# Attention kernel on one Trainium2 core: pairs of heads taken together, queries and keys turned by DMA instead of TensorE

## Chip, cores and metric

The kernel runs on 1 core of one Trainium2 chip. The metric is device time in microseconds (us) of the whole program, lower is better. The kernel before took 1261.8 us, the median of 3 runs (1261.73 to 1263.38).

## What is computed

One transformer block over 32 batches of 256 tokens by 128 channels, all in 32-bit floats, cut to what matters:

```
xn  = layernorm(x)
h   = rmsnorm(xn) * norm_w
q, k, v = h @ Wq, split(h @ Wkv)              # 16 heads of 64
q, k = head_rmsnorm(q, q_gamma), head_rmsnorm(k, k_gamma)
sim = tanh(q @ k.T / 50) * 50 * 64**-0.5      # per batch and head, 256 x 256
o   = softmax(sim) @ v
out = x + o @ Wo + ffn(xn)   # ffn: 512 hidden, gelu; W1 and W2 each get a
                             # rank-4 update that is made from 16 rows of xn
```

## The kernel before

The work is a software pipeline over the 32 batches. A step n (of 36, from -2 to 33) does the attention of batch n and, beside it, other stages of its neighbours: "load" of batch n+3, "turn" of n+2 (layer norm, transpose of x), "front" of n+1 (projections, head norms), "back" of n-1 (output products), "store" of n-2. Each engine runs its own fixed list of operations in order; semaphores join them, nothing else does. A step has 16 slots, one for each head, and the tables `AUX`, `VECTOR_STEPS`, `POOL_STEPS` and `Y_PRODUCTS` say which further work an engine takes in which slot.

- **Scores.** In each even slot TensorE computes the scores of a pair of heads (`scores`, L481): 12 matmuls, two at a time on 64 rows of the array each, three products of 16-bit high and low parts. The two heads have one PSUM bank each (`ps_scores`). A pair may overwrite them when both tanh of the pair before are done (`clamp_done`).
- **Softmax.** ScalarE takes tanh of one head, 512 columns (L555), then exp of the head before (L563). GpSimd makes the low part of the exponentials (`lo_part`, L905). `RING = 4` heads are buffered.
- **Values.** TensorE multiplies by the values three slots later (`values`, L503 to L505, 12 matmuls a head), into `ps_o`; VectorE divides by the sum (`divide`, L702 and L706).
- **Everything else** goes through three PSUM banks, `ps_aux`, which are handed out strictly in the order of `AUX`: entry i uses bank i mod 3, and TensorE fills it when the reader of entry i-3 is done (`wait_bank`). Entries are the projections "q", "k", "v" (4 each a batch, three matmuls of 512 columns, L406 to L408), the transposes of x ("xhT", "xnT", L427), of the attention output ("oT", L455) and of the normalised queries and keys ("qkT", 8 a batch, 4 transposes each, L448), the two low-rank updates "low" (L461) and the hidden layer "hid" (L466).
- **Readers.** ScalarE squares q (L575), and VectorE then scales it with gamma and so frees the bank (L729). ScalarE copies k (L580), oT (L588), and takes gelu of hid (L596), which needs a table load before it and one before the next exp. Of v, ScalarE makes the high part (L585) and VectorE the low part, which frees the bank (L734). The same for qkT: high part L591, low part L738, into `heads_T`. VectorE makes `w_eff` from low (L746).
- **Head norms.** GpSimd squares k (L880), VectorE sums (L667) and makes a seed, GpSimd runs three Newton turns (L893 to L899), VectorE multiplies q and k by the result in four instructions (`normalise`, L694).
- **Output.** 24 products a batch accumulate in `ps_y` (L523, L525), placed by `Y_PRODUCTS`; VectorE adds the rest (L716).
- **DMA.** SyncE (SP) issues all transfers: x twice (L384, L388), the rows of xn for the update as six small DMAs (L375), and the result (L395).

## Time and profile before

| | |
|---|---|
| median of 3 runs | 1261.8 us |
| the profiled execution's own time | 1261.8 us |
| its span, first to last instruction | 1259.8 us |
| busy share TensorE / weight loads / VectorE / ScalarE / GpSimd | 93 / 77 / 82 / 86 / 73% |
| granted TensorE clock, mean | 0.992 |
| mean busy share of the 16 DMA engines | 5% |

An engine's busy time is the union of its instructions. Matmuls overlap (a values matmul is shown as 0.19 us but the next starts 0.03 us later), so what TensorE's work takes is read from start to start. The same holds, by less, for the other engines: a 512-column activation is shown as 0.6 us and the next starts after 0.5. The clock column is 1.00 at 2.4 GHz and 0.50 at 1.2 GHz.

### The profile page before, as it was taken

The numbers are of one execution on the slowest core, as the hardware profiler recorded it, in microseconds if no ns is written. First come the engines' busy times: TensorE is split into PE (matmuls) and PEld (weight loads), VectorE is DVE, ScalarE is ACT, GpSimd is POOL, SyncE is SP. The second block draws the span as 40 slices with busy tenths as digits, with TensorE's granted clock in tenths as the row PEclk, the third lists the DMA queues.
The fourth block names the chain that finished last, engine by engine and source line by source line (L and its number), as shares of the span: only waits on it lengthen the run. The fifth ranks groups of instructions, "written<-read, shape, count | busy, mean of one in ns | idle before, by whom it ended". The sixth has DMA issues, their size and how long they took to land.

```text
span 1259.8 us, 36165 instructions
## 1 busy us (share of the span) xinstructions
PE 1165.6 (93%) x13897; PEld 972.3 (77%) x13897; DVE 1032.2 (82%) x2153; ACT 1082.2 (86%) x2055; POOL 917.6 (73%) x1105
## 2 busy tenths in 40 slices
PE   3789999999999999999999999999999999999988
PEld 2468887778877778878778878778878778878777
DVE  6788889888889888889888889888889888888862
ACT  3589898889898889888888988888988888988885
POOL 4477777777777777877777877777777777777663
PEclk9899999999999999999999999999999999999999
DMA  4000000000000000000000000000000000000000
GB/s 132 10 11 11 14 16 7 15 15 11 15 15 7 15 15 11 15 15 7 15 15 11 14 16 7 15 15 11 14 15 7 15 15 15 10 11 11 11 6 9
DMA packets 32224, 19.41 MB, mean 15 GB/s; under 512 B 3508, under 2 KB 31288, under 8 KB 32056
## 3 DMA queue, kind: packets, MB, share of 16 engines
q1 hardware_dynamic: 32056, 17.12, 4.7%
q8 instruction: 112, 1.84, 0.6%
q14 instruction: 56, 0.46, 0.1%
HBM read 12.13 MB, written 4.19 MB: 13 GB/s over the span
## 4 chain that ended last, share of the span: by engine, by line
PE 42%; DVE 25%; ACT 19%; issue 11%; POOL 1%; ACTq 0%; POOLq 0%
PE ps_scores L481 8%; ACT probs L563 6%; PE ps_aux L455 5%; DVE qk L729 4%; PE ps_aux L448 4%; PE ps_aux L406 4%; PE ps_y L525 4%; DVE heads_T L738 3%; DVE sel_rows L760 3%; DVE qk L694 3%; PE ps_aux L408 3%; PE ps_aux L407 3%; ACT L596 3%; DVE norm L667 3%; ACT hid L596 3%
## 5 line engine op out<-in xcount | busy, mean ns | idle before, releaser
L905 POOL TENSOR_TENSOR probs_lo<-probs 128x512 f16<-128x512 f32 x512 | 586.3, 1150 | 235.1 <-ACT probs L563 232.9
L555 ACT ACTIVATE clamped<-ps_scores 128x512 f32<-128x512 f32 x512 | 310.3, 606 | 124.5 <-PE ps_scores L481 124.4
L563 ACT ACTIVATE probs<-clamped 128x512 f32<-128x512 f32 x512 | 324.9, 635 | 0.4
L503 PE MATMUL ps_o<-v_hi,probs 128*128 128x65 bf16 x2048 | 240.0, 195 | 4.5 <-DVE o_sb L706 2.7
L504 PE MATMUL ps_o<-v_lo,probs 128*128 128x64 bf16 x2048 | 239.2, 193 | 0.0
L505 PE MATMUL ps_o<-v_hi,probs_lo 128*128 128x65 bf16 x2048 | 238.9, 194 | 0.0
L481 PE MATMUL ps_scores<-heads_T 64*128 64x256 f16 x3072 | 212.9, 271 | 14.2 <-ACT clamped L555 14.0
L406 PE MATMUL ps_aux<-w_hi,xhT_hi 128*128 128x512 f32 x384 | 191.5, 499 | 31.9 <-DVE qk L729 21.6
L503 PEld LDWEIGHTS ps_o<-v_hi,probs 128*128 128x128 bf16 x2048 | 192.1, 99 | 30.1 <-issue 18.2
L504 PEld LDWEIGHTS ps_o<-v_lo,probs 128*128 128x128 bf16 x2048 | 189.8, 99 | 5.0
L505 PEld LDWEIGHTS ps_o<-v_hi,probs_lo 128*128 128x128 f16 x2048 | 190.2, 98 | 0.0
L738 DVE TENSOR_TENSOR heads_T<-ps_aux,heads_T 128x512 f16<-128x512 f32 x256 | 169.6, 683 | 14.9 <-ACT heads_T L591 14.5
L448 PE MATMUL ps_aux<-ident,qk 128*128 128x128 f32 x1024 | 151.6, 282 | 19.9 <-DVE qk L694 19.9
L694 DVE TENSOR_TENSOR qk<-qk,rnorm 128x1024 f32<-128x1024 f32 x128 | 167.6, 1309 | 2.1 <-POOL rnorm L899 2.1
L481 PEld LDWEIGHTS ps_scores<-heads_T 64*128 64x128 f16 x3072 | 131.8, 94 | 40.1 <-issue 17.6
L525 PE MATMUL ps_y<-wo_sb,oT 128*128 128x128 f32 x1024 | 160.5, 275 | 0.0
L734 DVE TENSOR_TENSOR v_lo<-ps_aux,v_hi 128x512 bf16<-128x512 f32 x128 | 87.8, 686 | 81.1 <-ACT v_hi L585 81.1
L408 PE MATMUL ps_aux<-w_hi,xhT_lo 128*128 128x512 f32 x384 | 152.8, 398 | 0.0
L407 PE MATMUL ps_aux<-w_lo,xhT_hi 128*128 128x512 f32 x384 | 152.8, 398 | 0.0
L591 ACT CAST heads_T<-ps_aux 128x512 f16<-128x512 f32 x256 | 145.1, 593 | 7.6 <-PE ps_aux L448 5.8
L448 PEld LDWEIGHTS ps_aux<-ident,qk 128*128 128x128 f32 x1024 | 115.0, 143 | 46.6 <-issue 42.1
L525 PEld LDWEIGHTS ps_y<-wo_sb,oT 128*128 128x128 f32 x1024 | 143.3, 191 | 7.4 <-issue 0.4
(83 smaller groups left out, 2211.2 us busy)
## 6 DMA issues: line engine op xcount, KB each, us to landing
x_in<-in_L_attn_tokens_dram SPq DMA_DIRECT2D x32, 128.0 KB, 2.3
x_res<-in_L_attn_tokens_dram SPq DMA_DIRECT2D x32, 128.0 KB, 2.3
out_dram<-y_sb SPq DMA_DIRECT2D x32, 128.0 KB, 1.9
sel_raw<-xn SPq DMA_DIRECT2D x192, 4.0 KB
qk<-in_L_attn_Wkv_dram SPq DMA_DIRECT2D x2, 512.0 KB, 5.4
qk<-in_L_attn_Wq_dram SPq DMA_DIRECT2D x1, 512.0 KB, 3.6
qk<-in_L_ffn_W_dram SPq DMA_DIRECT2D x2, 256.0 KB
hid<-in_L_attn_q_gamma_dram SPq DMA_DIRECT2D x1, 512.0 KB, 7.0
```

What stands on the lines that cost most here:

```text
L406: pe.matmul(o, hi_l, hi_r, start=True, stop=False)
L448: ins = pe.transpose(bank[:, (j * TT + t) * P:(j * TT + t + 1) * P], qk[:, par, t, at:at + P], ident[:])
L481: ins = pe.matmul(ps_scores[:, odd, t * seq:(t + 1) * seq], heads_T[rows, pair, left, k, keys], heads_T[rows, pair, right, q], start=(i == ...
L503: pe.matmul(full, hi[:, col], v_hi[:, par, u, h], start=(u == 0), stop=False)
L504: pe.matmul(full[:, 0:DH], hi[:, col], v_lo[:, par, u, h], start=False, stop=False)
L505: ins = pe.matmul(full, probs_lo[:, buf, col], v_hi[:, par, u, h], start=False, stop=(u == TT - 1))
L525: ins = pe.matmul(o, oT[:, pair, tok], wo_sb[:, pair], start=False, stop=(i == n - 1))
L555: nc.scalar.activation(clamped[:, buf], ps_scores[:, s % SCORE_BANKS], ACT.Tanh).then_inc(clamp_done, 1)
L563: nc.scalar.activation(probs[:, buf], clamped[:, buf], ACT.Exp, bias=LIFT, scale=SOFTCLAMP * DH ** -0.5).then_inc(probs_done, 1)
L694: v.tensor_tensor(part, part, r.unsqueeze(3).to_broadcast([P, 2 * TT, 4, DH]), ALU.mult)\
L738: v.tensor_tensor(heads_T[:, k, 1].rearrange("p j t -> p (j t)"), bank, heads_T[:, k, 0].rearrange("p j t -> p (j t)"), ALU.subtract)\
L905: g.tensor_tensor(probs_lo[:, buf], probs[:, buf], probs[:, buf].bitcast(BF16)[:, 1::2], ALU.subtract).then_inc(lo_made, 1)
```

## The change

A step now has 8 slots, one for each pair of heads.

- `tanh`, `exp` and `lo_part` each take a whole pair, 1024 columns, in one instruction. `RING` is 2 pairs; `clamped` holds one pair. `values` of both heads comes two slots after their scores, ahead of the slot's other products instead of behind them.
- The "qkT" entries leave `AUX`: no transposes of q and k on TensorE, and no reads of their results. Instead ScalarE writes the 16-bit high part of a quarter of the normalised q and k (`half`, 1024 columns, from SBUF), VectorE the low part (`halves`, 1024 columns, two inputs in SBUF), and SP issues a transposing DMA for each (`turn_heads`), 256 KB, two for each of four chunks: 8 a batch. The scores of pairs 2c and 2c+1 wait for chunk c. `heads_T` has one buffer, `halves16` two.
- "xhT" and "xnT" become one entry "xT". Projections q and k of a batch are begun one step earlier (stage "turn" instead of "front"), the layer norm's statistics too.
- All orders are new: `AUX` has 21 entries, and ScalarE gets a list of its own, `SCALAR_STEPS`.
- SP's list: select rows in slot 1, store in slot 2, chunk 3 of the current batch in slot 3, chunks 0, 1, 2 of the next one in slots 5, 6, 7.

```diff
@@ -49,73 +49,63 @@
 
 AUX_BANKS = 3
 AUX = [
-    (1, "k", 0, 1), (1, "k", 1, 1), (1, "q", 2, 1),
-    (2, "qkT", 4, 0), (2, "qkT", 5, 0),
-    (3, "q", 3, 1),
-    (4, "oT", 0, -1), (4, "oT", 1, -1), (4, "k", 2, 1),
-    (5, "k", 3, 1), (5, "low", 0, 0), (5, "v", 0, 1),
-    (6, "oT", 2, -1), (6, "v", 1, 1),
-    (7, "oT", 3, -1), (7, "qkT", 6, 0),
-    (8, "qkT", 7, 0), (8, "v", 2, 1),
-    (9, "hid", 0, 0), (9, "hid", 1, 0),
-    (10, "low", 1, 0), (10, "v", 3, 1),
-    (11, "xhT", 0, 2),
-    (12, "qkT", 0, 1), (12, "qkT", 1, 1),
-    (13, "xnT", 0, 2),
-    (14, "q", 0, 2), (14, "qkT", 2, 1),
-    (15, "qkT", 3, 1), (15, "q", 1, 2),
+    (0, "k", 2, 1), (0, "k", 3, 1), (0, "oT", 0, -1),
+    (1, "v", 0, 1), (1, "v", 1, 1), (1, "oT", 1, -1),
+    (2, "low", 0, 0), (2, "v", 2, 1), (2, "v", 3, 1), (2, "oT", 2, -1),
+    (3, "xT", 0, 2), (3, "low", 1, 0), (3, "oT", 3, -1),
+    (4, "q", 0, 2), (4, "q", 1, 2),
+    (5, "hid", 0, 0), (5, "hid", 1, 0),
+    (6, "k", 0, 2), (6, "k", 1, 2),
+    (7, "q", 2, 2), (7, "q", 3, 2),
...
-RING = 4
-VALUES_LAG = 3
+RING = 2
+VALUES_LAG = 2
...
+SCALAR_STEPS = [
+    [("tanh",), ("q", 3, 1), ("exp",), ("k", 2, 1), ("k", 3, 1)],
+    [("tanh",), ("half", 3, 0), ("exp",), ("oT", 0, -1), ("v", 0, 1), ("v", 1, 1)],
+    [("tanh",), ("oT", 1, -1), ("exp",), ("v", 2, 1), ("v", 3, 1)],
+    [("tanh",), ("oT", 2, -1), ("exp",), ("xT", 0, 2)],
+    [("tanh",), ("oT", 3, -1), ("exp",), ("q", 0, 2), ("q", 1, 2)],
+    [("tanh",), ("half", 0, 1), ("exp",), ("hid", 0, 0), ("hid", 1, 0)],
+    [("tanh",), ("half", 1, 1), ("exp",), ("k", 0, 2), ("k", 1, 2)],
+    [("tanh",), ("half", 2, 1), ("exp",), ("q", 2, 2)],
+]
 VECTOR_STEPS = [
+    [("q", 2, 1), ("divide",), ("result",), ("q", 3, 1), ("sum", 2, 1), ("sum", 3, 1), ("sum", 4, 1)],
+    [("sum", 5, 1), ("norm_apply",), ("divide",), ("v", 0, 1), ("v", 1, 1)],
+    [("sum", 6, 1), ("sum", 7, 1), ("seed",), ("divide",), ("v", 2, 1), ("v", 3, 1)],
+    [("low", 0, 0), ("halves", 3, 0), ("divide",), ("low", 1, 0)],
+    [("xT", 0, 2), ("select",), ("divide",), ("normalise", 0, 1)],
+    [("q", 0, 2), ("q", 1, 2), ("divide",), ("normalise", 1, 1), ("halves", 0, 1)],
+    [("sum", 0, 2), ("sum", 1, 2), ("divide",), ("normalise", 2, 1), ("halves", 1, 1)],
+    [("normalise", 3, 1), ("divide",), ("norm_stats",), ("halves", 2, 1)],
 ]
 POOL_STEPS = [
+    [("rstd",), ("lo",)],
+    [("square", 2, 1), ("square", 3, 1), ("lo",)],
+    [("newton", 0), ("lo",)],
+    [("newton", 1), ("newton", 2), ("lo",)],
+    [("bias",), ("lo",)],
     [("lo",)],
...
+    [("square", 0, 2), ("square", 1, 2), ("lo",)],
 ]
+TURN_STEPS = {3: (3, 0), 5: (0, 1), 6: (1, 1), 7: (2, 1)}
+SELECT_SLOT = 1
+STORE_SLOT = 2
+Y_PRODUCTS = {2: 2, 3: 5, 4: 4, 5: 3, 6: 5, 7: 5}
...
+        halves16 = sb("halves16", [P, 2, 2, PAIRS // CHUNKS, TT * 2, P], F16)
+        heads_T = sb("heads_T", [P, 2, PAIRS, TT, 2, P], F16)
-        clamped = sb("clamped", [P, RING, TT * seq])
-        probs = sb("probs", [P, RING, TT * seq])
-        probs_lo = sb("probs_lo", [P, RING, TT * seq], F16)
+        clamped = sb("clamped", [P, 2, TT * seq])
+        probs = sb("probs", [P, RING, 2, TT * seq])
+        probs_lo = sb("probs_lo", [P, RING, 2, TT * seq], F16)
...
+        def chunk_of(par, c):
+
+            return qk[:, par].rearrange("p t (j n) -> p (t j) n", j=2)[:, :, c * 4 * DH:(c + 1) * 4 * DH]\
+                .rearrange("p b (a n) -> p a b n", n=P)
...
+            def turn_heads(st, c, ahead):
+
+                b, _, _ = st.batch(ahead)
+                wait(sp, scores_done, 2 * PAIRS * (b - 1) + 4 * c + 4)
+                for half, made in enumerate((half_hi_made, half_lo_made)):
+                    sp.wait_ge(made, CHUNKS * b + c + 1)
+                    sp.dma_start(heads_T[:, half, 2 * c:2 * c + 2].rearrange("p a t j n -> p (a t j) n"),
+                                 halves16[:, c % 2, half].rearrange("p a b n -> p (a b n)"),
+                                 transpose=True).then_inc(heads_turned[c], 16)
...
-                elif kind == "qkT":
-
-                    if k % 2 == 0:
-                        wait(pe, qk_normed, 4 * b + k // 2 + 1)
-                    for j in range(2):
-                        for t in range(TT):
-                            at = j * HEADS * DH + k * P
-                            ins = pe.transpose(bank[:, (j * TT + t) * P:(j * TT + t + 1) * P],
-                                               qk[:, par, t, at:at + P], ident[:])
...
             def scores(st, pair):
 
                 b, par, _ = st.batch(0)
-                wait(pe, qkT_split, PAIRS * b + pair + 1)
-                wait(pe, clamp_done, HEADS * b + 2 * pair)
+                if pair % 2 == 0:
+                    wait(pe, heads_turned[pair // 2], 32 * (b + 1))
+                wait(pe, clamp_done, PAIRS * b + pair)
                 hi, lo, q, k = 0, 1, 0, 1
                 for t in range(TT):
-                    keys = slice(t * P, (t + 1) * P)
                     for i, (left, right) in enumerate(((hi, hi), (lo, hi), (hi, lo))):
                         for odd in range(2):
                             rows = slice(DH * odd, DH * odd + DH)
                             ins = pe.matmul(ps_scores[:, odd, t * seq:(t + 1) * seq],
-                                            heads_T[rows, pair, left, k, keys], heads_T[rows, pair, right, q],
+                                            heads_T[rows, left, pair, t, k], heads_T[rows, right, pair, :, q],
                                             start=(i == 0), stop=(i == 2))
...
+            def values(st, ahead, pair):
...
-                        col = slice(u * seq + t * P, u * seq + (t + 1) * P)
-                        pe.matmul(full, hi[:, col], v_hi[:, par, u, h], start=(u == 0), stop=False)
-                        pe.matmul(full[:, 0:DH], hi[:, col], v_lo[:, par, u, h], start=False, stop=False)
-                        ins = pe.matmul(full, probs_lo[:, buf, col], v_hi[:, par, u, h],
...
-                    if "attn" in st.stages and s % 2 == 0:
-                        scores(st, s // 2)
-                    for task in aux_tasks(st, s, PER_BATCH):
+                for s in range(PAIRS):
+                    if "attn" in st.stages:
+                        scores(st, s)
+                    late = pair_of(st, s, VALUES_LAG)
+                    if late:
+                        values(st, *late)
+                    for task in aux_tasks(st, s):
                         aux(st, *task)
                     if "back" in st.stages and s in Y_PRODUCTS:
                         result(st, sum(Y_PRODUCTS.get(i, 0) for i in range(s)), Y_PRODUCTS[s])
...
+            def tanh(st, pair):
+                b, _, _ = st.batch(0)
+                wait(act, scores_done, 2 * PAIRS * b + 2 * pair + 2)
+                wait(act, probs_done, PAIRS * b + pair)
+                nc.scalar.activation(clamped[:].rearrange("p j n -> p (j n)"),
+                                     ps_scores[:].rearrange("p j n -> p (j n)"), ACT.Tanh).then_inc(clamp_done, 1)
+
+            def exp(st, pair):
+                b, _, _ = st.batch(0)
+                wait(act, clamp_done, PAIRS * b + pair + 1)
+                wait(act, attended, PAIRS * b + pair + 1 - RING)
+                nc.scalar.activation(probs[:, pair % RING].rearrange("p j n -> p (j n)"),
+                                     clamped[:].rearrange("p j n -> p (j n)"), ACT.Exp, bias=LIFT,
+                                     scale=SOFTCLAMP * DH ** -0.5).then_inc(probs_done, 1)
+
+            def half(st, c, ahead):
+                b, par, _ = st.batch(ahead)
+                act.wait_ge(qk_normed, CHUNKS * b + c + 1)
+                wait(act, heads_turned[(c + 2) % CHUNKS], 32 * (b + c // 2))
+                nc.scalar.copy(halves16[:, c % 2, 0], chunk_of(par, c)).then_inc(half_hi_made, 1)
...
+            def halves(st, c, ahead):
+
+                b, par, _ = st.batch(ahead)
+                dve.wait_ge(half_hi_made, CHUNKS * b + c + 1)
+                v.tensor_tensor(halves16[:, c % 2, 1], chunk_of(par, c), halves16[:, c % 2, 0], ALU.subtract)\
+                    .then_inc(half_lo_made, 1)
...
+            def lo_part(st, pair):
+                b, _, _ = st.batch(0)
+                buf = pair % RING
+                pool.wait_ge(probs_done, PAIRS * b + pair + 1)
+                g.tensor_tensor(probs_lo[:, buf].rearrange("p j n -> p (j n)"), probs[:, buf].rearrange("p j n -> p (j n)"),
+                                probs[:, buf].rearrange("p j n -> p (j n)").bitcast(BF16)[:, 1::2],
                                 ALU.subtract).then_inc(lo_made, 1)
 
```

In `AUX` and the lists the last number is the batch relative to the step's. Entry by entry the banks of the new `AUX` are: slot 0 k2, k3, oT0 in banks 0, 1, 2; slot 1 v0, v1, oT1 in 0, 1, 2; slot 2 low0, v2, v3, oT2 in 0, 1, 2, 0; slot 3 xT, low1, oT3 in 1, 2, 0; slot 4 q0, q1 in 1, 2; slot 5 hid0, hid1 in 0, 1; slot 6 k0, k1 in 2, 0; slot 7 q2, q3 in 1, 2.

## Rows read from the trace of the kernel before

**Rows 1.** The page's first part: busy time of each engine, its share of the span, instructions.

```profile
PE 1165.6 (93%) x13897; PEld 972.3 (77%) x13897; DVE 1032.2 (82%) x2153; ACT 1082.2 (86%) x2055; POOL 917.6 (73%) x1105
```

**Rows 2.** Timeline of GpSimd, its once-a-batch addition: start us, us, instruction.

```profile
134.38 1.72 POOL L912 TENSOR_TENSOR x_b<-x_res,b_bc 128x256 f32<-128x256 f32 x1
...
1151.89 1.72 POOL L912 TENSOR_TENSOR x_b<-x_res,b_bc 128x256 f32<-128x256 f32 x1
```

**Rows 3.** Groups by line: count | busy us, mean ns | idle before, releaser.

```profile
L905 POOL TENSOR_TENSOR probs_lo<-probs 128x512 f16<-128x512 f32 x512 | 586.3, 1150 | 235.1 <-ACT probs L563 232.9
L563 ACT ACTIVATE probs<-clamped 128x512 f32<-128x512 f32 x512 | 324.9, 635 | 0.4
L555 ACT ACTIVATE clamped<-ps_scores 128x512 f32<-128x512 f32 x512 | 310.3, 606 | 124.5 <-PE ps_scores L481 124.4
...
L694 DVE TENSOR_TENSOR qk<-qk,rnorm 128x1024 f32<-128x1024 f32 x128 | 167.6, 1309 | 2.1 <-POOL rnorm L899 2.1
...
L746 DVE SCALAR_TENSOR_TENSOR w_eff<-ps_aux,scale_col,w1T 128x512 f32<-128x512 f32 x32 | 23.7, 742 | 0.3 <-PE ps_aux L461 0.3
...
L603 ACT CAST w_hi<-qk 128x1024 fp32r<-128x1024 f32 x3 | 3.0, 1044 | 5.6 <-DVE qk L824 5.6
```

**Rows 4.** Timeline of TensorE in one step: start us, us, instruction.

```profile
608.48 0.50 PE L406 MATMUL ps_aux<-w_hi,xhT_hi 128*128 128x512 f32 x1
...
609.29 0.60 PE L448 MATMUL ps_aux<-ident,qk 128*128 128x128 f32 x4
609.72 0.39 PE L525 MATMUL ps_y<-wo_sb,oT 128*128 128x128 f32 x2
609.95 0.19 PE L503 MATMUL ps_o<-v_hi,probs 128*128 128x65 bf16 x1
...
610.31 0.63 PE L448 MATMUL ps_aux<-ident,qk 128*128 128x128 f32 x4
...
616.75 0.83 PE L481 MATMUL ps_scores<-heads_T 64*128 64x256 f16 x12
617.51 1.09 PE L448 MATMUL ps_aux<-ident,qk 128*128 128x128 f32 x8
```

**Rows 5.** Timeline of ScalarE around the gelu of one step.

```profile
633.57 0.62 ACT L555 ACTIVATE clamped<-ps_scores 128x512 f32<-128x512 f32 x1
634.05 0.65 ACT L563 ACTIVATE probs<-clamped 128x512 f32<-128x512 f32 x1
634.72 1.28 ACT L596 ACT_TABLE_LOAD   x1
636.02 1.57 ACT L596 ACTIVATE hid<-ps_aux,b_col 128x256 f32<-128x256 f32 x4
637.53 0.60 ACT L555 ACTIVATE clamped<-ps_scores 128x512 f32<-128x512 f32 x1
```

**Rows 6.** Timeline of VectorE in one step.

```profile
618.80 0.68 DVE L729 TENSOR_TENSOR qk<-ps_aux,g_bc 128x512 f32<-128x512 f32 x1
619.40 1.28 DVE L738 TENSOR_TENSOR heads_T<-ps_aux,heads_T 128x512 f16<-128x512 f32 x2
```

**Rows 7.** TensorE by stretches: length, busy (x), PEclk, DMA share, GB/s.

```profile
70.00:75.00 5.00, 3.89 (x58) 1.00 0.18 52
75.00:79.00 4.00, 2.80 (x24) 0.71 0.00 0
```

**Rows 8.** Timeline of TensorE inside the second of those stretches.

```profile
75.67 0.83 PE L481 MATMUL ps_scores<-heads_T 64*128 64x256 f16 x12 [1.78 <-ACT clamped L555]
77.03 1.94 PE L448 MATMUL ps_aux<-ident,qk 128*128 128x128 f32 x8 [0.53 <-DVE qk L694]
```

**Rows 9.** Timeline of SP: the issue of the six small row DMAs of one step.

```profile
613.15 3.99 SPq L375 DMA_DIRECT2D sel_raw<-xn  x6
```

**Rows 10.** DMA issues: KB each, median us from issue to landing.

```profile
x_in<-in_L_attn_tokens_dram SPq DMA_DIRECT2D x32, 128.0 KB, 2.3
qk<-in_L_attn_Wq_dram SPq DMA_DIRECT2D x1, 512.0 KB, 3.6
```

More of the change, by code:

```diff
@@ L288, in block_kernel @@
         v_split = sem("v_split")
-        qkT_hi_made = sem("qkT_hi_made")
-        qkT_split = sem("qkT_split")
+        half_hi_made = sem("half_hi_made")
+        half_lo_made = sem("half_lo_made")
+        heads_turned = [sem(f"heads_turned{c}") for c in range(CHUNKS)]
         oT_copied = sem("oT_copied")
@@ L322, in wait_bank, with aux_tasks, bank_of, pair_of @@
                     return
[L324 removed]
+        def aux_tasks(st, slot):
             for i, (s, kind, k, ahead) in enumerate(AUX):
[L326 removed]
+                if s == slot and STAGE[ahead] in st.stages:
                     yield i, kind, k, ahead
[L329 to L331 removed]
+        def bank_of(kind, k):
+            i = [(what, n) for _, what, n, _ in AUX].index((kind, k))
+            return ps_aux[:, i % AUX_BANKS, :]
+        def pair_of(st, slot, lag):
+            ahead, pair = (0, slot - lag) if slot >= lag else (-1, slot - lag + PAIRS)
             there = "attn" if ahead == 0 else "back"
[L333 removed]
+            return (ahead, pair) if there in st.stages else None
+        def chunk_of(par, c):
+            return qk[:, par].rearrange("p t (j n) -> p (t j) n", j=2)[:, :, c * 4 * DH:(c + 1) * 4 * DH]\
+                .rearrange("p b (a n) -> p a b n", n=P)
         def run_all(eng, run):
@@ new lines, in run @@
+            def run(st):
+                for s in range(PAIRS):
+                    for what, *k in SCALAR_STEPS[s]:
+                        if what == "tanh":
+                            if "attn" in st.stages:
+                                tanh(st, s)
+                        elif what == "exp":
+                            if "attn" in st.stages:
+                                exp(st, s)
+                        elif STAGE[k[1]] in st.stages:
+                            if what == "half":
+                                half(st, *k)
+                            else:
+                                aux(st, what, *k)
@@ L616, in _, with norm_stats @@
             v.memset(v_hi[:, :, :, :, DH:DH + 1], 1.0)
-            def norm_stats(st):
-                b, par, half = st.batch(2)
+            def norm_stats(st, ahead):
+                b, par, half = st.batch(ahead)
                 dve.wait_ge(x_loaded[par], 16 * (half + 1))
@@ L726, in aux @@
                     if k == 0:
-                        wait(dve, aux_filled["qkT"], PAIRS * (b - 1))
+                        wait(dve, half_hi_made, CHUNKS * (b - 1))
                     t, c = k // 2, k % 2
@@ L872, in _, with square @@
             pool.wait_ge(masks_made, 6)
-            def square(st, k):
-                b, par, _ = st.batch(1)
+            def square(st, k, ahead):
+                b, par, _ = st.batch(ahead)
                 t, c = k // 2, 2 + k % 2
```

306 lines of the change are left out of this document (121 added, 185 removed).

## The prediction

> **What bounds the kernel now.** The page's first part comes first: TensorE is busy for 93% of the span, and no other engine is over 86% [rows 1]. A once-a-batch instruction gives the period: 27 batches between its two starts, so (1151.89 - 134.38) / 27 = 37.7 us each [rows 2]. The groups by line show who waits: tanh waits 124.5 us in all for the scores, 3.9 us a batch, while GpSimd's 235.1 us of waiting before its low parts holds nobody up [rows 3]. The reader is to see a kernel bound by TensorE's list, with ScalarE close behind.
>
> **What is removed.** Eight qkT entries a batch leave TensorE. Each is four transposes, 609.29 to 609.72, 0.43 us from start to start [rows 4]: 3.4 us a batch. ScalarE's fixed part is saved 16 times. A 512-column tanh is shown as 606 ns and a 1024-column copy as 1044 [rows 3], so 512 more columns cost 438 ns, while a second instruction would cost 0.48 (633.57 to 634.05 [rows 5]); 0.05 us saved each time, 0.8 us a batch. If only these terms counted, the period would fall to about 34 us.
>
> **What is added.** ScalarE's four half copies replace eight casts (4 x 0.93 against 8 x 0.48, no change), VectorE's four subtractions with both inputs in SBUF take 1.31 us each if they are like normalise [rows 3], against 8 x 0.60 [rows 6]: 0.4 us more, beside other work. GpSimd's low parts become 2 us pieces in place of 1; a pair's has more than a slot until its values, so nothing for it. SP gets 8 large DMAs, behind and ahead of its loads.
>
> **The new order is what decides.** I follow one step at TensorE's full clock, from the start of one pair's tanh to the next. Start-to-start costs: tanh 0.91 (0.48 + 0.43), exp 0.95, half copy 0.93, any 512-column ScalarE operation 0.48 (0.60 until its result can be used) [rows 3, 5]; 12 scores matmuls 0.76, or 0.83 to their end, q, k or v 0.81, four transposes 0.43, an output product (two matmuls) 0.23, values of a pair 2 x 0.36 [rows 4]; VectorE 0.60 for 512 columns, 0.68 to the result [rows 6], w_eff 0.74 [rows 3]. Handovers between engines I put at 0.2 us an interval, an estimate. An interval is the longest chain that the lists force:
> - 0 to 1: tanh, square of q3 (0.60), VectorE's scaling (0.68), which frees bank 2 for oT0 (0.43), scores 1 (0.83): 3.6 with handovers.
> - 1 to 2: tanh, half 3, exp, copy of oT0 (0.60), only then oT1 in the same bank, scores 2: 0.91 + 0.93 + 0.95 + 0.60 + 0.43 + 0.83 + 0.2 = 4.9.
> - 2 to 3: oT2 needs bank 0, which low0 holds until VectorE's first operation of slot 3, behind its v3, which is behind ScalarE's v3, its last of slot 2. Tanh 0.91, oT1 0.48, exp 0.95, v2 0.48, v3 0.60, VectorE's v3 0.60, w_eff 0.74, oT2 0.43, two products 0.46, scores 3 0.83, handovers 0.2: 6.7 us. TensorE has nothing to do for 2.6 of them, from the end of v3's matmuls to oT2.
> - 3 to 4: tanh, copy of oT2, oT3, five products (1.15), scores 4: 4.1.
> - 4 to 5, on TensorE: values, q0, q1, four products, scores: 0.72 + 1.62 + 0.92 + 0.76 = 4.0.
> - 5 to 6, on ScalarE: tanh, half 0, exp with its tail 1.05, table load 1.30, four gelu 1.51 [rows 5]: 5.7.
> - 6 to 7: tanh, half 1 with its tail 1.04, table load 1.30, exp, k0, k1: 5.2.
> - 7 to 0: tanh, half 2, exp, q2: 3.3.
>
> The sum is 3.6 + 4.9 + 6.7 + 4.1 + 4.0 + 5.7 + 5.2 + 3.3 = 37.5 us, against 37.7 now. The freed TensorE time turns into waits, for ScalarE in intervals 1, 5, 6, 7 and for VectorE in 2. That is 0.2 x 32 = 6 us less; filling the pipeline costs about 4 more (half copy 0.9, subtraction 1.3 and a DMA of about 2 between the first normalise and the first scores). At full clock the new kernel is level with the old one, near 1260 us.
>
> **The clock.** TensorE will idle 3.4 - 0.2 = 3.2 us more a batch, and 2.6 us of that at once. In the kernel before TensorE was busy 3.89 of 5 us, with one wait of 1.78 for a tanh, when the granted clock fell; the next 4 us have a mean of 0.71, that is partly the 1.2 GHz level, and eight transposes took 1.94 us there against 1.09 at 2.4 GHz [rows 4, 7, 8]. The new stall is longer than that wait, and is in every batch, so I expect a fall in nearly every batch. What follows it is all on the chain: oT2, products, scores 3, then oT3, products, scores 4, values, q0. A mean of 0.71 over 4 us is 0.58 of them, 2.3 us, at half clock, in which half of the work is done: a fall costs about 1.2 us where it lies on the chain. The same eight transposes give 0.85. I take 1.2, with 0 and two falls, 2.4, as the ends. The forecast is 37.5 + 1.2 = 38.7 us a batch: 1262 + 1.0 x 32 + 4, about 1298 us. The sum is made against the profiled execution's own time, 1261.8 us, which is 2.0 over its span and equal to the median.
>
> **The transposing DMAs.** No row shows one. Eight a batch fit if each takes less than 37.5 / 8 = 4.7 us of the queue; the tightest is chunk 0, whose low half is ready about 7 us before its scores. The nearest rows: 128 KB land in 2.3 us and 512 KB in 3.6 [rows 10], which gives about 3 us for 256 KB, hidden. The upper end: if SP issued each 128 x 128 block as a DMA of its own, at the 3.99 / 6 = 0.67 us of the six small ones [rows 9], the 64 blocks of a batch would take 42.6 us. I take the lower, since the transfer is issued as one of large rows.
> The Trainium skill has both ends too. "VectorE: DVE Perf Modes", section "The three transpose paths", gives 1309 ns for a 128 x 128 block by DMA against 390 on TensorE, a rule against this change: one block after the other would be 64 x 1.309 = 84 us a batch, an estimate from that page, and a kernel of over 2500 us; that is rival C with another price. "DMA: Bandwidth & Descriptors", section "Latency and other measured facts", gives 261 GB/s for a transposing DMA, 1 us of movement for 256 KB. No run here shows either yet.
>
> **Rivals.**
> - A, the clock stays up. For it: the steady stretch before had waits and no fall. Then 37.3 to 37.8 us a batch, 1252 to 1272 us, centre 1262.
> - B, faster. One mechanism: oT2 does not wait, because VectorE reads low0 before ScalarE's v3. Then interval 2 is bound by TensorE (values 0.72, low 0.05, v2 and v3 1.6, oT2 0.43, two products 0.46, scores 0.83: 4.1 us) and not 6.7, the clock has no long stall to fall on, and the kernel takes 1262 - 2.4 x 32 + 4, near 1190 us; with half of it, 1225. It decides at whether w_eff of low0 is made before v3's low part. Against it: the lists place it behind.
> - C, the DMA queue bounds. Transfers or their issue take more than 4.7 us each; at the 42.6 us above, 1262 + 4.9 x 32 = about 1420 us. Scores would wait for `heads_turned` in every second slot, and SP would be late with x.
> - D, contention: VectorE's subtractions with two SBUF inputs and GpSimd slow each other. No row parts them; the spread from 0.60 us for 512 columns with one input in PSUM [rows 6] to 1.31 for 1024 from SBUF [rows 3] leaves 0.1 us an instruction for it. If the v splits came 0.5 us later, interval 2 would grow by as much: 16 us on top of the forecast, inside the range.
>
> **How the numbers follow.** A measurement of this kernel can tell about 0.2% (2.5 us) from no change. Forecast with D 0.47, A 0.22 (0.07 faster, 0.07 same, 0.08 slower), B and its partial forms 0.22, C 0.09. Faster 0.29, same 0.07, slower 0.64. The range: the clock's cost from 0 to two falls a batch (up to 1262 + 2.4 x 32) gives 1340 at the top; at the bottom it reaches into B, to 1205. It leaves out C and the strongest form of B, together under 0.2. The likeliest case alone is 1275 to 1325.
>
> **What would show it.** Right: a period near 38.7 us; TensorE's busy share down to about 85%; tanh of 1024 columns near 1.04 us; w_eff of low0 as what ends TensorE's longest steady wait, about 2.6 us before oT2; a mean clock near 0.95, with falls once a batch right after that wait; scores not waiting for a DMA. Wrong: a period under 37, or no wait before oT2 (B); clock 0.99 (A); scores released by DMA or SP (C).

## The result: 16% slower, and the profile after

The changed kernel takes 1461.7 us, the median of 4 runs (1459.6 to 1462.6), against 1262.5 for the kernel before. The ratio is 1.158, 95% interval 1.156 to 1.160. The forecast was 1298, its range ended at 1340: the sign was right, the size was not.

The page of the kernel after: the busy shares, the engines' shares of the chain that ended last, and the issue row of the new DMAs (median us to landing).

```profile
PE 1157.2 (79%) x12873; PEld 878.1 (60%) x12873; DVE 1227.3 (84%) x2025; ACT 1031.6 (71%) x1415; POOL 917.9 (63%) x849
...
DVE 56%; PE 19%; ACT 18%; issue 6%; POOL 1%; DMA 0%; DVEq 0%; ACTq 0%; POOLq 0%
...
heads_T<-halves SPq DMA_TRANSPOSE x256, 3.1
```

VectorE executes 128 instructions fewer than before [rows 1] and is busy 195 us more. The chain is mostly its own. TensorE fell to 79%, ScalarE to 71%, and the DMAs are not on the chain. The groups by line say which instructions grew:

```profile
L926 POOL TENSOR_TENSOR probs_lo<-probs 128x1024 f16<-128x1024 f32 x256 | 516.7, 2019 | 406.8 <-ACT probs L563 406.8
L719 DVE TENSOR_TENSOR halves<-qk,halves 128x1024 f16<-128x1024 f32 x128 | 274.6, 2145 | 1.2 <-ACT halves L571 1.2
L712 DVE TENSOR_TENSOR qk<-qk,rnorm 128x1024 f32<-128x1024 f32 x128 | 247.0, 1930 | 0.0
L754 DVE TENSOR_TENSOR qk<-ps_aux,g_bc 128x512 f32<-128x512 f32 x128 | 84.4, 678 | 6.1 <-ACT sq_q L582 6.1
L776 DVE CAST sel_rows<-sel_raw 72x256 f16<-72x256 f32 x32 | 36.1, 1127 | 0.0
```

`normalise` (L712) is the same instruction as before and went from a mean of 1309 ns [rows 3] to 1930. The new subtraction (L719), which I had put at 1310, is 2145. The scaling of q (L754), which reads PSUM, is at the 0.68 us of [rows 6].

The waits say who pays (engine and line, what it waited for: us in all, times, longest):

```profile
PE ps_aux L418 <- DVE qk L754: 123.2, 33, 4.4
PE ps_aux L459 <- DVE w_eff L766: 74.7, 31, 2.5
```

The second is the wait before oT2 that the prediction had named, at 2.4 us a time. The first is the larger one, and the prediction has no such wait.

The period, from GpSimd's timeline (the once-a-batch instruction of [rows 2]; seven batches lie between the two rows):

```profile
206.25 0.78 POOL L934 TENSOR_TENSOR x_b<-x_res,b_bc 128x256 f32<-128x256 f32 x1
...
516.34 0.78 POOL L934 TENSOR_TENSOR x_b<-x_res,b_bc 128x256 f32<-128x256 f32 x1
```

310.09 / 7 = 44.3 us, against 37.7 before and 38.7 forecast. From tanh to tanh one step reads as follows, in us, beside the prediction's intervals; this step is one of the longer ones, so the means of 26 steps stand below it, and those of e2, the kernel without the low part (see the experiments):

| interval | 0-1 | 1-2 | 2-3 | 3-4 | 4-5 | 5-6 | 6-7 | 7-0 |
|---|---|---|---|---|---|---|---|---|
| predicted, full clock | 3.6 | 4.9 | 6.7 | 4.1 | 4.0 | 5.7 | 5.2 | 3.3 |
| after, one step | 8.8 | 4.9 | 8.3 | 4.2 | 4.0 | 6.4 | 5.2 | 3.3 |
| after, mean | 8.7 | 4.9 | 7.8 | 4.2 | 4.0 | 6.4 | 5.2 | 3.3 |
| e2, mean | 3.9 | 4.9 | 7.8 | 4.5 | 4.0 | 5.7 | 5.2 | 3.3 |

Five of eight are right to 0.1 us. The loss on the mean is in 0 to 1 (5.1), 2 to 3 (1.1) and 5 to 6 (0.7). Interval 2 to 3 is as long in e2, so the low part has no share in that one; what makes it longer than 6.7 is told under "The clock" below.

**What happens in 0 to 1.** VectorE's timeline (start us, us, instruction):

```profile
618.65 1.22 DVE L719 TENSOR_TENSOR halves<-qk,halves 128x1024 f16<-128x1024 f32 x1
619.78 2.92 DVE L712 TENSOR_TENSOR qk<-qk,rnorm 128x1024 f32<-128x1024 f32 x1
...
624.54 0.16 DVE L656 TENSOR_SCALAR var_eps<-mean_var 128x2 f32<-128x2 f32 x1
624.61 2.92 DVE L719 TENSOR_TENSOR halves<-qk,halves 128x1024 f16<-128x1024 f32 x1
627.45 0.68 DVE L754 TENSOR_TENSOR qk<-ps_aux,g_bc 128x512 f32<-128x512 f32 x1
```

GpSimd's over the same time:

```profile
619.37 2.25 POOL L926 TENSOR_TENSOR probs_lo<-probs 128x1024 f16<-128x1024 f32 x1 [4.59 <-ACT probs L563]
621.58 3.02 POOL L901 TENSOR_TENSOR sq_k<-qk 128x512 f32<-128x512 f32 x2
624.56 1.89 POOL L926 TENSOR_TENSOR probs_lo<-probs 128x1024 f16<-128x1024 f32 x1
626.41 1.99 POOL L866 TENSOR_TENSOR rstd<-var_eps,minus_half 128x4 f32<-128x4 f32 x1
```

And TensorE's:

```profile
623.87 0.40 PE L420 MATMUL ps_aux<-w_hi,xhT_lo 128*128 128x512 f32 x1
628.19 0.50 PE L418 MATMUL ps_aux<-w_hi,xhT_hi 128*128 128x512 f32 x1 [3.92 <-DVE qk L754]
628.53 0.59 PE L419 MATMUL ps_aux<-w_lo,xhT_hi 128*128 128x512 f32 x1
628.91 0.63 PE L420 MATMUL ps_aux<-w_hi,xhT_lo 128*128 128x512 f32 x1
```

Read the first two together. GpSimd's low part begins at 619.37 while VectorE's subtraction runs: it takes 2.25 us, not 1.89. VectorE's normalise begins at 619.78, takes 2.92 us and not 1.22, and ends at 622.70, which is 1.08 after the low part's end. GpSimd's squares come next and take 3.02 in place of 2 x 1.04: 0.94 too long, about what was left of the normalise. At 624.61 the subtraction begins 0.05 us behind a low part, and takes 2.92 again. So the two engines take turns, and the later one waits for the rest of the other's instruction. The scaling of q2 comes behind that, at 627.45; it frees the bank that k3 needs, and TensorE has waited 3.92 us. Its next matmuls show 0.59 and 0.63 us instead of 0.39: the fall of the clock comes on top. TensorE by stretches, as in [rows 7], has it at a mean of 1.00 before and of 0.86 after:

```profile
600.00:622.00 22.00, 20.74 (x259) 16.78 (x257) 19.75 (x26) 19.21 (x27) 12.14 (x14) 1.00 0.33 58
622.00:646.00 24.00, 16.31 (x173) 11.10 (x170) 18.64 (x39) 13.27 (x20) 18.27 (x20) 0.86 0.35 65
```

(Busy us of TensorE, weight loads, VectorE, ScalarE and GpSimd, then the clock, the DMA share and GB/s.)

The Trainium skill has this rule, and the prediction had passed over it. "SBUF — State Buffer", section "SBUF: two separate sides", says that VectorE and GpSimd share one pair of SBUF ports as an exclusive lock held for the whole instruction, which a VectorE instruction needs when it has two SBUF inputs or runs in a mode that uses both ports. The trace agrees: L712 and L719, with two SBUF inputs, are stretched by up to 1.7 us, L754 with one input in PSUM never (692 ns at most).

### The profile page after: what moved, and what is told of

Read it like the earlier page. It is cut to its first block, busy times and chain, and to the rows that moved or that the text cites. A ratio compares the mean times of both kernels' runs of the same rounds, so it can differ in the third digit from the quotient of the medians.

```text
span 1457.8 us, 32774 instructions
## 1 busy us (share of the span) xinstructions
PE 1157.2 (79%) x12873; PEld 878.1 (60%) x12873; DVE 1227.3 (84%) x2025; ACT 1031.6 (71%) x1415; POOL 917.9 (63%) x849
## 3 DMA queue, kind: packets, MB, share of 16 engines
q1 hardware_dynamic: 302392, 84.26, 31.2%
## 4 chain that ended last, share of the span: by engine, by line
DVE 56%; PE 19%; ACT 18%; issue 6%; POOL 1%; DMA 0%; DVEq 0%; ACTq 0%; POOLq 0%
DVE qk L712 16%; DVE halves L719 14%; PE ps_scores L485 7%; ACT probs L563 7%; PE ps_aux L459 6%; DVE qk L754 4%; ACT clamped L556 4%; ACT oT L595 4%; DVE v_lo L759 3%; DVE o_sb L731 3%; DVE norm L685 3%; DVE sel_rows L776 2%; DVE sel_rows L780 2%; PE ps_y L527 2%; DVE w_eff L766 2%
## 5 line engine op out<-in xcount | busy, mean ns | idle before, releaser
L926 POOL TENSOR_TENSOR probs_lo<-probs 128x1024 f16<-128x1024 f32 x256 | 516.7, 2019 | 406.8 <-ACT probs L563 406.8
L556 ACT ACTIVATE clamped<-ps_scores 128x1024 f32<-128x1024 f32 x256 | 264.0, 1031 | 259.4 <-PE ps_scores L485 259.0
L719 DVE TENSOR_TENSOR halves<-qk,halves 128x1024 f16<-128x1024 f32 x128 | 274.6, 2145 | 1.2 <-ACT halves L571 1.2
L563 ACT ACTIVATE probs<-clamped 128x1024 f32<-128x1024 f32 x256 | 273.7, 1069 | 0.6
L712 DVE TENSOR_TENSOR qk<-qk,rnorm 128x1024 f32<-128x1024 f32 x128 | 247.0, 1930 | 0.0
L418 PEld LDWEIGHTS ps_aux<-w_hi,xhT_hi 128*128 128x128 f32 x384 | 77.6, 202 | 199.8 <-DVE qk L754 137.9
L459 PE MATMUL ps_aux<-ident,o_sb 128*128 128x128 f32 x512 | 104.6, 339 | 106.6 <-DVE w_eff L766 74.7
L901 POOL TENSOR_TENSOR sq_k<-qk 128x512 f32<-128x512 f32 x128 | 161.8, 1284 | 19.6 <-ACT qk L587 17.7
L459 PEld LDWEIGHTS ps_aux<-ident,o_sb 128*128 128x128 f32 x512 | 67.3, 167 | 162.4 <-DVE w_eff L766 88.1
L571 ACT CAST halves<-qk 128x1024 f16<-128x1024 f32 x128 | 134.5, 1051 | 24.4 <-DVE qk L712 22.1
```

The costliest lines, as they stand in the source:

```text
L418: pe.matmul(o, hi_l, hi_r, start=True, stop=False)
L459: ins = pe.transpose(bank[:, (j * TT + t) * P:(j * TT + t + 1) * P], o_sb[:, par, t, at:at + P], ident[:])
L556: nc.scalar.activation(clamped[:].rearrange("p j n -> p (j n)"), ps_scores[:].rearrange("p j n -> p (j n)"), ACT.Tanh).then_inc(clamp_done, 1)
L563: nc.scalar.activation(probs[:, pair % RING].rearrange("p j n -> p (j n)"), clamped[:].rearrange("p j n -> p (j n)"), ACT.Exp, bias=LIFT, ...
L712: v.tensor_tensor(part, part, r.unsqueeze(3).to_broadcast([P, 2 * TT, 4, DH]), ALU.mult)\
L719: v.tensor_tensor(halves16[:, c % 2, 1], chunk_of(par, c), halves16[:, c % 2, 0], ALU.subtract)\
```

## The experiments

The kernel before, beside each: 1262.7 to 1263.0 us. "Low part" is GpSimd's `lo_part`.

| kernel | us | ratio (95%) | L719 ns | L712 ns | clock |
|---|---|---|---|---|---|
| after | 1461.7 | 1.156 to 1.160 | 2145 | 1930 | 0.925 |
| e1: low part 2 x 512 | 1315.8 | 1.038 to 1.043 | 1526 | 1303 | 0.964 |
| e2: no low part | 1304.2 | one run | 1228 | 1218 | 0.957 |
| e3: no transposition | 1461.5 | one run | 2145 | 1939 | 0.92 |
| e4: low0 early | 1406.7 | 1.111 to 1.116 | 2275 | 1906 | 0.931 |
| e5: e1 and e4 | 1257.8 | 0.995 to 0.998 | 1629 | 1249 | 0.993 |
| e10: e4, low part 4 x 256 | 1246.9 | 0.986 to 0.989 | 1501 | 1362 | 0.986 |

**e1, the low part in two pieces.** The same work in instructions half as long:

```diff
-                g.tensor_tensor(probs_lo[:, buf].rearrange("p j n -> p (j n)"), probs[:, buf].rearrange("p j n -> p (j n)"),
-                                probs[:, buf].rearrange("p j n -> p (j n)").bitcast(BF16)[:, 1::2],
-                                ALU.subtract).then_inc(lo_made, 1)
+                for at in range(0, 1024, 512):
+                    part = slice(at, at + 512)
+                    ins = g.tensor_tensor(probs_lo[:, buf].rearrange("p j n -> p (j n)")[:, part],
+                                          probs[:, buf].rearrange("p j n -> p (j n)")[:, part],
+                                          probs[:, buf].rearrange("p j n -> p (j n)").bitcast(BF16)[:, 1::2][:, part],
+                                          ALU.subtract)
+                ins.then_inc(lo_made, 1)
```

> Only change to the changed kernel: GpSimd's low part of a pair is made by two instructions of 512 columns instead of one of 1024. Theory P (port): a VectorE instruction with two inputs in SBUF (the subtractions halves, normalise) that meets a running GpSimd instruction waits until it has ended, so 1.22 us becomes up to 2.92 with a GpSimd instruction of 1.89 us. Then the longest should be about 1.22 + 1.0 = 2.2 us, the means of halves and normalise should fall from 2145 and 1930 ns to about 1700, and the batch should be 2 to 4 us shorter: 1340 to 1400 us. Theory D (the transposing DMAs slow VectorE's SBUF traffic): durations and time unchanged, 1455 to 1470. Theory C (the clock alone): unchanged durations, time within 10 us of 1461.

1315.8 us: 146 us less, more than I had expected. GpSimd has more to do (its group is 636.5 us in all, against 516.7), and the kernel is far faster. The subtraction's shortest, median and longest, in ns, first in the kernel after, then in e1:

```profile
L719 DVE TENSOR_TENSOR halves<-qk,halves x128: 1209/1761/2926, 45.2 to 1425.3; 128x1024 f16<-128x1024 f32 x128
```

```profile
L719 DVE TENSOR_TENSOR halves<-qk,halves x128: 1210/1325/2096, 44.2 to 1282.1; 128x1024 f16<-128x1024 f32 x128
```

The shortest stays, and the longest falls by 0.83 us, close to the 0.85 by which a piece became shorter (1.89 to 1.04).

**e2, no low part.** GpSimd subtracts 8 columns of 1024; for the rest the values are made with a low part of zero, set once at the start.

```diff
+            g.memset(probs_lo[:].rearrange("p r j n -> p (r j n)"), 0.0)
...
-                g.tensor_tensor(probs_lo[:, buf].rearrange("p j n -> p (j n)"), probs[:, buf].rearrange("p j n -> p (j n)"),
-                                probs[:, buf].rearrange("p j n -> p (j n)").bitcast(BF16)[:, 1::2],
+                g.tensor_tensor(probs_lo[:, buf, 0, 0:8], probs[:, buf, 0, 0:8],
+                                probs[:, buf, 0].bitcast(BF16)[:, 1:16:2],
                                 ALU.subtract).then_inc(lo_made, 1)
```

> Leaves out: the low part of the exponentials, of which GpSimd makes only 8 columns a pair (the rest of the buffer is zero). All semaphores, DMAs and other work stay. Theory P: hardly any VectorE instruction meets a long GpSimd one; halves and normalise fall to about 1.22 to 1.4 us, the interval from tanh 0 to tanh 1 falls from 8.8 to about 4 us, and the kernel takes what the chain of the prediction gives, 37.5 to 39 us a batch: 1260 to 1310 us. Theory D: the DMAs are all there, so halves stays near 2.1 us and the time above 1430. Theory C: the stalls of TensorE stay, time above 1430.

1304.2 us. This is close to the kernel that I had predicted: hardly an instruction is stretched, the period is 39.2 us (tanh 1 at 638.06 and 677.25), and the intervals are 3.9, 4.9, 7.4 to 8.3, 4.2, 4.0, 5.7, 5.2, 3.3. The groups by line of this kernel:

```profile
L719 DVE TENSOR_TENSOR halves<-qk,halves 128x1024 f16<-128x1024 f32 x128 | 157.2, 1228 | 68.3 <-ACT halves L571 68.3
L712 DVE TENSOR_TENSOR qk<-qk,rnorm 128x1024 f32<-128x1024 f32 x128 | 155.9, 1218 | 0.0
```

So 157 of the 199 us go with the low part, and all but 12 of those with its length of 1024. VectorE's busy time falls from 1227 to 982 us with it, while the values had hardly waited for the low part (3.7 us in all in the kernel after); so the loss is what it does to VectorE and to GpSimd's other instructions. All 256 transposing DMAs are still there, so these are not what stretches VectorE's instructions.

**e3, the DMAs without transposition.** The same 256 KB, copied straight; the scores are then made from untransposed data.

```diff
-                    sp.dma_start(heads_T[:, half, 2 * c:2 * c + 2].rearrange("p a t j n -> p (a t j) n"),
-                                 halves16[:, c % 2, half].rearrange("p a b n -> p (a b n)"),
-                                 transpose=True).then_inc(heads_turned[c], 16)
+                    sp.dma_start(heads_T[:, half, 2 * c:2 * c + 2].rearrange("p a t j n -> p (a t j n)"),
+                                 halves16[:, c % 2, half].rearrange("p a b n -> p (a b n)")).then_inc(heads_turned[c], 16)
```

> Leaves out: the transposition; the same 256 KB move by a plain DMA with the same waits and semaphores, so the scores are of wrong data. Theory P: VectorE's durations and the time stay, 1450 to 1470 us. Theory D: halves and normalise fall to about 1.3 us and the time to 1260 to 1320. If SP's list of slow transposing issues held something up, the time would fall by that without a change in VectorE's durations.

1461.5 us, no change, though the copy lands after 2.3 us in place of 3.1 and the queue's share of the 16 engines falls from 31.2 to 16.4%. The transposition costs nothing here, and rival C falls.

**e4, w_eff of low0 ahead of the low parts of v2 and v3** (rival B's mechanism, made on purpose), and **e5**, e4 together with e1:

```diff
-    [("sum", 6, 1), ("sum", 7, 1), ("seed",), ("divide",), ("v", 2, 1), ("v", 3, 1)],
-    [("low", 0, 0), ("halves", 3, 0), ("divide",), ("low", 1, 0)],
+    [("sum", 6, 1), ("sum", 7, 1), ("seed",), ("divide",), ("low", 0, 0), ("v", 2, 1), ("v", 3, 1)],
+    [("halves", 3, 0), ("divide",), ("low", 1, 0)],
```

> Only change: VectorE makes w_eff from low0 ahead of the low parts of v2 and v3 in slot 2, not after them in slot 3, so bank 0 comes free for oT2 earlier. The step of the prediction that it tests: interval 2 to 3 is the chain through v3 and low0. If right, that interval (8.3 us in the changed kernel) falls by 1.5 to 3 us and the wait of TensorE's oT2 for w_eff (74.7 us in all) is gone: 1375 to 1415 us. If the stall were hidden by something else that is late at the same time, under 20 us are gained.

> Both mends together: low part in two instructions of 512 columns, and w_eff of low0 ahead of the v low parts. Theory P with the chain of the prediction: the chain of interval 2 to 3 is then the one through oT1 and v3 alone (about 4.5 us in place of 7.4 to 8.3), the long stall of TensorE and the clock's fall behind it go, and VectorE (86% busy with the first mend alone) is the next bound: 1235 to 1275 us, about level with the kernel before. If the port were the only loss left, the second mend would add under 15 us: above 1300.

e4: 1406.7, 55 us less; interval 2 to 3 goes from a mean of 7.8 to 5.2, while 5 to 6 grows from 6.4 to 7.1. e5: 1257.8, 58 less than e1 and 149 less than e4. The two effects add up: making w_eff early is worth 55 to 58 us with long pieces or short ones, the pieces 146 to 149 in either order. TensorE's wait for w_eff does not go altogether: 74.7 us in all become 23.0 in e4, and 75.9 (e1) become 39.5 in e5, where interval 2 to 3 is 6.1 and not the 4.5 that I had named. e5's intervals are 4.3, 4.9, 6.1, 4.2, 4.0, 5.7, 5.2, 3.3, 37.5 us in all; its clock is 0.993, so hardly a fall is left to pay. It beats the kernel before by 5 us.

**e6 and e12, the kernel before with late low parts.** e6 makes the low part once a pair with 1024 columns, e12 at the same moment in two instructions of 512. Both follow the second head's exp, so the first head's is later than before.

```diff
+                if h % 2 == 0:
+                    return
                 pool.wait_ge(probs_done, HEADS * b + h + 1)
-                g.tensor_tensor(probs_lo[:, buf], probs[:, buf], probs[:, buf].bitcast(BF16)[:, 1::2],
-                                ALU.subtract).then_inc(lo_made, 1)
+                for one in (buf - 1, buf):
+                    ins = g.tensor_tensor(probs_lo[:, one], probs[:, one], probs[:, one].bitcast(BF16)[:, 1::2],
+                                          ALU.subtract)
+                ins.then_inc(lo_made, 1)
```

This is e12; e6 has both buffers in one `tensor_tensor`. In both the values of the first head wait for the pair's low part too.

> The kernel before with one part of the change alone: GpSimd makes the low part of a pair in one instruction of 1024 columns, after the second head's exp; everything else is as before. Theory P: normalise (mean 1309 ns before, longest 2027) now meets instructions twice as long and has cases up to about 2.9 us; its mean rises to 1450 to 1900 ns, and the kernel is 5 to 60 us slower, part of which is that the first head's low part is made later. Theory that only the new order or the DMAs matter: mean of normalise within 60 ns of 1309.

> The kernel before with the low parts of both heads of a pair made after the second head's exp, as in the 1024-column version of 1366.0 us, but still as two instructions of 512 columns. Theory that most of those 103 us are the later low part (the values wait for it three slots behind, where they waited for nothing): 1330 to 1370 us. Rival, that the 1024-column instruction's hold on VectorE made them: 1262 to 1290 us, and normalise back near 1309 ns.

e6: 1366.0 (ratio 1.081 to 1.084), well beyond what I had expected; e12: 1397.9, above the 1330 to 1370 of its own expectation. The kernel before cannot be used to price the long piece: the later moment costs 135 us without it, and with it the kernel is even 32 us faster, although normalise is stretched more (mean 1619 ns against 1464 in e12 and 1309 before). The long piece takes 1.89 us where two short ones take 2.08; that this is why was not tried. So e6 is no price of the lock, and the theory that I gave it was mis-sized. The waits of e12 show it:

```profile
PE ps_o L503 <- POOL probs_lo L908: 118.5, 98, 3.1
```

**e7, e1 with 20 filler matmuls ahead of oT2**, into unused columns of `ps_y`, to keep TensorE busy in its stall:

```diff
+                if kind == "oT" and k == 2:
+                    wait(pe, y_added, st.batch(-1)[0])
+                    for _ in range(20):
+                        pe.matmul(ps_y[:, 384:512], w_hi[:, 0:P], w_hi[:, 0:P], start=True, stop=True)
```

> The changed kernel with the low part in two instructions, and 20 more matmuls of 128 columns (their results unused, into free columns of ps_y) just ahead of oT2, where TensorE waits for w_eff of low0. They do nothing but keep TensorE busy during that wait. Theory C (the clock falls because of this stall, and the fall costs on the chain): the granted clock rises from 0.964 to 0.98 or more, interval 2 to 3 shrinks from about 7.8 towards 6.9 us, and the kernel gains 10 to 35 us on the 1316 of the kernel without them: 1280 to 1306. If the falls come from other stalls or cost nothing on the chain: clock within 0.01 of 0.964, time 1310 to 1325.

1305.7 us, 10 less than e1, and the clock 0.987 instead of 0.964. TensorE in the same stretch, first e1, then e7:

```profile
200.00:1200.00 1000.00, 862.34 (x10175) 669.74 (x10173) 891.00 (x1597) 806.50 (x1114) 763.67 (x858) 0.97 0.37 66
```

```profile
200.00:1200.00 1000.00, 908.43 (x10803) 716.56 (x10800) 924.83 (x1619) 818.64 (x1129) 799.92 (x877) 1.00 0.37 67
```

So the falls follow this stall, as predicted, and go with it. Their price is read behind the stall, on the mean of 26 steps: from the start of oT2 to tanh 3 it takes 2.61 us in e1 and 1.93 in e7, and interval 3 to 4 takes 4.45 and 4.15. That is 1.0 us a batch, near the 1.2 of the prediction. The whole kernel gains only 0.3 us a batch, for two reasons. Intervals 0 to 1 and 5 to 6 are 0.3 us longer together (L719 rose from 1526 to 1638 ns), so the period falls from 39.6 to 39.0. And from the last tanh to the end e7 takes 21.5 us, against 15.1 in e1. The starts of tanh 1 give the period, 26 batches apart, first in e1, then in e7:

```profile
210.22 1.03 ACT L556 ACTIVATE clamped<-ps_scores 128x1024 f32<-128x1024 f32 x1 [0.88 <-PE ps_scores L485]
...
1238.92 1.02 ACT L556 ACTIVATE clamped<-ps_scores 128x1024 f32<-128x1024 f32 x1 [0.43 <-PE ps_scores L485]
```

```profile
209.98 1.02 ACT L560 ACTIVATE clamped<-ps_scores 128x1024 f32<-128x1024 f32 x1 [0.87 <-PE ps_scores L489]
...
1223.88 1.02 ACT L560 ACTIVATE clamped<-ps_scores 128x1024 f32<-128x1024 f32 x1 [0.87 <-PE ps_scores L489]
```
No run of one reaches into those of the other: e1's lowest is 1310.2, e7's highest 1306.7.

**e8, e1 with tanh and exp in two instructions of 512 each:**

```diff
-                nc.scalar.activation(clamped[:].rearrange("p j n -> p (j n)"),
-                                     ps_scores[:].rearrange("p j n -> p (j n)"), ACT.Tanh).then_inc(clamp_done, 1)
+                nc.scalar.activation(clamped[:, 0], ps_scores[:, 0], ACT.Tanh)
+                nc.scalar.activation(clamped[:, 1], ps_scores[:, 1], ACT.Tanh).then_inc(clamp_done, 1)
...
```

The exp is cut in the same way.

> The changed kernel with the low part in two instructions, and tanh and exp in two instructions of 512 columns each too, one after the other: undoes the other half of the merging. The prediction priced the merging at 0.05 us an instruction saved, 0.8 us a batch: if right, 10 to 35 us slower than the 1316 of the kernel without it. If ScalarE's start-to-start cost were hidden by its waits, under 8 us.

1319.8 us (1318.6 to 1322.2), 4 us more than e1, whose own runs spread over 8: merging ScalarE's instructions is worth next to nothing here.

**e9 and e11, the scaling of q2 ahead of the subtraction of half 2**, in the kernel after (e9) and in e5 (e11):

```diff
-    [("q", 2, 1), ("divide",), ("result",), ("q", 3, 1), ("sum", 2, 1), ("sum", 3, 1), ("sum", 4, 1)],
+    [("divide",), ("result",), ("q", 3, 1), ("sum", 2, 1), ("sum", 3, 1), ("sum", 4, 1)],
...
-    [("normalise", 3, 1), ("divide",), ("norm_stats",), ("halves", 2, 1)],
+    [("normalise", 3, 1), ("divide",), ("norm_stats",), ("q", 2, 2), ("halves", 2, 1)],
```

> The changed kernel with one VectorE entry moved: the scaling of q2 stands in slot 7 ahead of the subtraction of half 2, and no longer first in the next slot 0. Theory: the 8.8 us from tanh 0 to tanh 1 are k3's wait for the bank that q2 holds, behind a stretched normalise 3 and a stretched subtraction of half 2; with q2 ahead of one of the two, 1.5 to 3 us of that interval go, 1360 to 1420 us against 1461. Rival: VectorE has so little left over (84% busy, 90% once low0 was moved) that the subtraction, now behind q2, holds up the division and q3 by as much: over 1440 us.

> The version of 1257.8 us (low part in two pieces of 512, w_eff of low0 early) with the scaling of q2 moved ahead of the subtraction of half 2 as well. Theory: the bank of q2 comes free about 1 us earlier, and as TensorE waits for ScalarE's tanh and oT there too, a part of it shows: 1235 to 1256 us. Rival: that interval is then bound by ScalarE and the move gives nothing, 1255 to 1262 us.

e9: 1458.6 (1456.6 to 1459.0), hardly a change; e11: 1294.7, 37 us more than e5. k3 gets its bank sooner, but the subtraction now stands ahead of the scaling of q3, which frees the bank of oT0, the next transposes, and these are what scores 1 wait behind. TensorE's timeline of e9 and, in the second fence, its waits in e11:

```profile
622.72 0.50 PE L418 MATMUL ps_aux<-w_hi,xhT_hi 128*128 128x512 f32 x1 [1.07 <-DVE qk L754]
...
626.45 1.11 PE L459 MATMUL ps_aux<-ident,o_sb 128*128 128x128 f32 x4 [2.77 <-DVE qk L754]
```

```profile
PE ps_aux L459 <- DVE qk L754: 68.4, 30, 2.3
```

For e9 the rival was right, that the subtraction holds up q3 by as much; for e11 both cases were too low. Both show TensorE waiting for whichever scaling stands behind the subtraction; an order with the subtraction behind both of them was not tried.

**e10, four pieces of 256**, with low0 early (`range(0, 1024, 256)` in e5):

> The changed kernel with GpSimd's low part in four pieces of 256 columns and w_eff of low0 ahead of v2's and v3's low parts (the version of 1257.8 us has two pieces of 512). Theory that a VectorE instruction waits for the rest of the GpSimd instruction then running and for no more: the wait halves with the piece; the subtraction of a half falls from 1629 ns to 1350 to 1500, and the kernel takes 1235 to 1256 us. Rival: what counts is GpSimd's share of busy time and not the length of a piece: the subtraction stays at 1600 ns or more, and the fixed part of twice as many instructions makes the kernel slower, 1260 to 1290 us.

1246.9 us, ratio 0.986 to 0.989: the best kernel here, 15.8 us below the kernel before. Its groups by line and waits:

```profile
L928 POOL TENSOR_TENSOR probs_lo<-probs 128x256 f16<-128x256 f32 x1024 | 787.1, 798 | 52.3 <-ACT probs L563 52.3
...
PE ps_o L507 <- POOL probs_lo L928: 76.0, 95, 3.5
PE ps_aux L459 <- DVE w_eff L766: 43.8, 31, 1.4
```

L719 is at 1501 ns, just over the 1350 to 1500 I had named, and L712 rose from 1249 to 1362, so the wait of these two did not halve: above 1222 ns they have 279 and 140 ns here, 407 and 27 in e5. VectorE's busy time fell from 1146 us (e5) to 1076 all the same, since others are held up less too (the layer norm's L667 for xn: 821 to 642 ns). The rival, that GpSimd's share of busy time counts and not the length of a piece, does not hold: the share rose from 80 to 90% and the kernel became faster. The price is on the other side: the values now wait for GpSimd. Shorter pieces than these were not tried.

## Why the prediction was wrong, step by step

- **The step that failed** is in "What is added": four subtractions at 1.31 us, "0.4 us more, beside other work", and with it rival D, "no row parts them ... leaves 0.1 us an instruction". The mechanism had been named and its price taken from a mean. Measured, each is 2145 ns, and the four normalise with them 1930: (2145 - 1222 + 1930 - 1222) x 4 = 6.5 us a batch of VectorE's time, and 7.7 with the small instructions (VectorE is busy 1227 us, against 982 in e2, over 32 batches). "GpSimd's low parts become 2 us pieces in place of 1 ... so nothing for it" was true of GpSimd's own time and missed what the length does to its neighbour. On the path it fell where the prediction had no wait: its 0 to 1 begins at tanh and goes through q3, at 3.6 us, while k3 waited for the bank of q2, behind a stretched normalise and a stretched subtraction. The mean was 8.7 us, against 3.9 in e2.
- **A row did part them.** One line's instructions of the kernel before and of the one after, with the shortest, median and longest in ns; first before:

```profile
L694 DVE TENSOR_TENSOR qk<-qk,rnorm x128: 1215/1222/2027, 41.4 to 1222.7; 128x1024 f32<-128x1024 f32 x128
L912 POOL TENSOR_TENSOR x_b<-x_res,b_bc x32: 727/1719/1719, 96.7 to 1247.3; 128x256 f32<-128x256 f32 x32
```

then after:

```profile
L934 POOL TENSOR_TENSOR x_b<-x_res,b_bc x32: 723/782/786, 116.1 to 1446.8; 128x256 f32<-128x256 f32 x32
L776 DVE CAST sel_rows<-sel_raw x32: 280/1207/1215, 39.4 to 1398.0; 72x256 f16<-72x256 f32 x32
```

  The addition of [rows 2], on which I had read the period, takes 0.73 us at its shortest and took 1.72 there, in the kernel before already. It began at 134.38, and VectorE was then inside this normalise:

```profile
134.17 1.33 DVE L694 TENSOR_TENSOR qk<-qk,rnorm 128x1024 f32<-128x1024 f32 x1
```

  The 0.99 us too many are about what was left of it. Normalise itself has a median of 1222 ns and a longest of 2027; the mean of 1309 [rows 3], which I took for its price, hides that. The lock can be bounded from it: 2 us pieces against 1.2 us instructions make up to 1.9 us a hit, and eight large VectorE instructions a batch are exposed. That upper end, 8 x 1.9 = 15 us a batch, belonged into the range.
- **The chain of intervals was nearly right**, with the low part away. 37.5 us at full clock and 38.7 with the clock's part were forecast; e2 gives 39.2, and 1304 us against the forecast of 1298. Its 0 to 1 is 0.3 longer than predicted. In 2 to 3 oT2 starts 4.97 us after tanh 2, in e2 and in the kernel after alike, and from there to tanh 3 it takes 1.93 at full clock (e7): 6.9, where I had 6.7. (e5's sum is 37.5 as well, but by another way: 0.7 more in 0 to 1 and 0.6 less in 2 to 3.)
- **The clock** fell after the stalls (mean 0.925 and not 0.95, as there are more stalls). Its price of 1.2 us a batch behind the wait before oT2 was about right: above 1.93 us from oT2 to tanh 3, and 4.15 in 3 to 4, e2 has 0.9 and 0.4 on the mean, e1 0.7 and 0.3, and the kernel after 0.9 and nothing. What the fall behind the other stall, in 0 to 1, costs the kernel after by itself was not tried.
- **Rival B** had the right place: with the order that it names, most of that stall goes, and 55 to 58 us with it. I had put 108 between B and the forecast, but interval 2 ends at 5.2 (e4) to 6.1 (e5) and not at 4.1, and in e4 interval 5 to 6 gives 0.7 us of it back. It did not happen here because the lists place w_eff behind v3's low part, as the text said.
- **Rival C** fell: a transposing DMA lands in 3.1 us, as taken from [rows 10]. "VectorE: DVE Perf Modes" of the Trainium skill, section "The three transpose paths", gives 1309 ns a block; eight blocks one after the other would be 10.5 us a DMA, an estimate from that page, and the row does not show that. e3, without the transposition, takes the same time.
- **Removed terms:** TensorE's saving turned into waits, as said; ScalarE's 0.8 us a batch is real at most for 4 us in all (e8).
